# Recurrent kernel, one core: the next step's x gate goes into the PSUM sum from ScalarE in two halves, and no longer from VectorE

## The reference, cut to what matters

```
x = x + L0(x, cond)                      # gate, see below
xw = einsum('ntd,dh->nth', x, Wx) + b
def step(h_prev, xw_t):
    h_next = tanh(xw_t + h_prev @ Wh)    # 512 steps, one after the other
    return h_next, h_next
x = x + L1(x)                            # all h of the scan
x = x + L2(x)                            # forget/input gates f, i, candidate c, two cumulative sums over time
x = x + L3(x, ...)                       # one 512x512 product and a rank-8 term for each sequence
```

## Time and profile before

| | us |
|---|---|
| median of 3 runs | 1370.43 |
| lowest and highest | 1368.74, 1372.99 |
| the profiled execution, its own time | 1372.59 |
| its span, first to last instruction | 1370.7 |
| PE busy in the span | 1340.4 |
| DVE busy | 1066.7 |
| POOL busy | 767.2 |
| ACT busy | 695.2 |

### The profile page before, as it was taken

One profiled execution on the slowest core, in us unless ns is written; L12 is line 12 of the kernel. 1 busy time (PEld: TensorE's weight loads), 2 busy tenths in 40 slices (PEclk: granted clock), 3 DMA queues, 4 the chain that ended last, 5 costly groups with the idle time before them and its releaser, 6 DMA issues. The chain is left out here.

```text
span 1370.7 us, 50350 instructions
## 1 busy us (share of the span) xinstructions
PE 1340.4 (98%) x21246; PEld 887.3 (65%) x21246; DVE 1066.7 (78%) x2912; ACT 695.2 (51%) x2228; POOL 767.2 (56%) x620
## 2 busy tenths in 40 slices
PE   8999999999999999999999999999999997999998
PEld 6656666666666666666666666666666644677776
DVE  5756878777777777777777787878777888998993
ACT  4388555555555555555555555555545442333332
POOL 3255655464646464545555555554535557887884
PEclk9999999999999999999999999999999998999999
DMA  9771333333434242424242424241416568999993
GB/s 374 271 264 37 64 65 64 64 64 68 69 63 71 57 78 55 74 56 72 56 80 54 81 49 80 48 72 26 71 25 119 143 146 167 330 325 335 329 323 119
DMA packets 442276, 168.13 MB, mean 123 GB/s; under 512 B 406449, under 2 KB 409649, under 8 KB 438850
## 3 DMA queue, kind: packets, MB, share of 16 engines
q1 hardware_dynamic: 441584, 164.53, 47.6%
q10 hardware_dynamic: 466, 0.38, 0.1%
HBM read 96.72 MB, written 68.16 MB: 120 GB/s over the span
## 5 line engine op out<-in xcount | busy, mean ns | idle before, releaser
L509 PEld LDWEIGHTS recb<-hs,scanS 128*128 128x128 f16 x16352 | 466.1, 96 | 148.2 <-DVE hs L1492 144.3
L509 PE MATMUL recb<-hs,scanS 128*128 128x32 f16 x16352 | 488.3, 176 | 4.6 <-DVE hs L1492 3.5
L763 ACT ACTIVATE hs<-pre 128x64 f16<-128x64 f32 x512 | 131.2, 256 | 489.0 <-DVE pre L1480 487.5
L1480 DVE TENSOR_REDUCE pre<-recb 128x64 f32<-128x128 f32 x511 | 148.9, 291 | 186.4 <-PE recb L509 184.3
L1295 DVE RECIPROCAL gates<-gates 128x64 f32<-128x64 f32 (+1 forms) x484 | 257.8, 555 | 0.4
L1053 POOL TENSOR_SCALAR hbuf<-hbuf,sup 128x512 f32<-128x512 f32 (+2 forms) x61 | 94.1, 1542 | 126.9 <-ACT hbuf L767 126.9
L1492 DVE TENSOR_TENSOR hs<-konst,hs 128x64 f16<-128x64 f32 x512 | 103.5, 202 | 61.5 <-ACT konst L764 49.5
L1068 POOL TENSOR_TENSOR xt<-xt,pout 128x512 f32<-128x512 f32 x64 | 75.5, 1179 | 126.4 <-DVE pout L1325 126.4
L1335 DVE TENSOR_TENSOR recb<-xw,recb 128x128 f32<-128x128 f32 x511 | 145.8, 285 | 0.1
L1061 POOL TENSOR_TENSOR gates<-gates 128x512 f32<-128x512 f32 x62 | 78.8, 1271 | 105.0 <-DVE gates L1295 103.7
L767 ACT ACTIVATE hbuf<-pre 128x64 f32<-128x64 f32 x512 | 122.5, 239 | 0.0
(11 more groups left out here) (252 smaller groups left out, 2725.7 us busy)
## 6 DMA issues: line engine op xcount, KB each, us to landing
xt<-in_x SPq DMA_DIRECT2D x64, 256.0 KB, 3.5
g_d<-gst SPq DMA_DIRECT2D x64, 256.0 KB, 4.2
n_d<-nst SPq DMA_DIRECT2D x64, 256.0 KB, 3.1
x_d<-xt SPq DMA_DIRECT2D x64, 256.0 KB, 3.3
out<-gates SPq DMA_DIRECT2D x63, 256.0 KB, 4.9
xt<-x_d SPq DMA_DIRECT2D x28, 512.0 KB, 6.1
stage<-in_w SPq DMA_DIRECT2D x11, 1024.0 KB, 6.8
xt<-g_d SPq DMA_DIRECT2D x14, 512.0 KB, 8.0
```

The lines of the kernel that those rows point to most:

```text
L509: last = nc.tensor.matmul(sums[t % 2][:, m].rearrange("p a b -> p (a b)"), w[:, k, m * P:(m + 1) * P], hs[:, k].rearrange("p a b -> p (a b ...
L763: nc.scalar.activation(hs[:, :, 0, :], pre[t % 2][:], ACT.Tanh, scale=unscale).then_inc(s_h, 1)
L1480: nc.vector.tensor_reduce(pre[t % 2][:], sums[t % 2].rearrange("p c a b -> p c b a"), axis=AX.X, op=ALU.add).then_inc(s_pre, 1)
```

## The change

ScalarE gets a function `seed(n)`, called between its second and its third tanh of step n - 1. It writes half the gate of step n into both halves of the sum region (an ACTIVATE with Copy and scale 0.5), so their sum is again the gate, and raises a new semaphore `s_seed`. PE's step waits for it behind `s_hs`. VectorE's `seed`, the pair `halves`, its two memsets and their semaphore go. The input products of a block (`input_products`, chunk 0) get a wait that the gates they overwrite have been read. The seed waits, once in most blocks, for DVE's read of `bounds` in the same bank.

```diff
             def step(j, t):
                 pe.wait_ge(s_hs, TS * j + t + 1)
+                pe.wait_ge(s_seed, TS * j + t)
...
         @block.scalar
+            def seed(n):
+                if n == T:
+                    return
+                if n == 1:
+                    act.wait_ge(s_rec, 1)
+                if n % TS == 0:
+                    act.wait_ge(s_xw, C * (n // TS + 1))
+                if n - 1 == BOUND_FIRST:
+                    act.wait_ge(s_bd, 1)
+                elif n - 1 == BOUND_C:
+                    act.wait_ge(s_bd, 9)
+                elif TS < n < T - 2 * TS and (n - 1) % TS == BOUND_STEP:
+                    act.wait_ge(s_bd, 8 * (n // TS + 1) + 1)
+                gate = xw[n // TS % 2][:, n % TS].unsqueeze(2).to_broadcast([P, C, 2, B])
+                nc.scalar.activation(sums[n % 2], gate, ACT.Copy, scale=0.5).then_inc(s_seed, 1)
+
             def tanh(j, t):
...
                 nc.scalar.activation(hps, pre[t % 2][:], ACT.Tanh, scale=unscale).then_inc(s_h, 1)
+                seed(TS * j + t + 1)
                 if t % OCT == 0 and o >= RING:
                     act.wait_ge(s_x2, o - RING + 1)
                 nc.scalar.activation(hbuf[:, t % (RING * OCT)], pre[t % 2][:], ACT.Tanh, scale=unscale).then_inc(s_hb, 1)
...
             def input_products(q, m):
                 act.wait_ge(s_xp, C * q + m + 1)
                 if q >= 2 and m == 0:
+                    act.wait_ge(s_seed, TS * (q - 1) - 1)
                     act.wait_ge(s_bd, known(q) if q > 2 else 8)
...
         @block.vector
-            def seed(j, t):
-                j, t = j + t // TS, t % TS
-                if j == NBLK:
-                    return
-                if t == 0 and j:
-                    dve.wait_ge(s_xw, C * (j + 1))
-                gate = xw[j % 2][:, t].unsqueeze(2).to_broadcast([P, C, 2, B])
-                keep = halves.unsqueeze(1).unsqueeze(3).to_broadcast([P, C, 2, B])
-                nc.vector.tensor_tensor(sums[t % 2], gate, keep, ALU.mult)
...
                         nc.vector.tensor_tensor(pre[0][:], xw[0][:, 0], h0wh[:], ALU.add).then_inc(s_pre, 1)
-                        dve.wait_ge(s_rec, 1)
-                        nc.vector.memset(halves[:, 0:1], 1.0)
-                        nc.vector.memset(halves[:, 1:2], 0.0).then_inc(s_halves, 1)
-                        dve.wait_ge(s_halves, 1)
                     else:
                         dve.wait_ge(s_rec, TS * j + t + 1)
                         nc.vector.tensor_reduce(pre[t % 2][:], ...).then_inc(s_pre, 1)
-                    seed(j, t + 1)
```

More of the change, by code:

```diff
@@ L174, in build @@
         turned = recb[:, 2 * P:3 * P]
-        halves = recb[:, 2 * P:2 * P + 2]
         by_batch = turned.rearrange("p (c b) -> p c b", c=C)[:, :, 0:B]
@@ L224, in build @@
                                     "s_hyp s_lr").split())
-        (s_x1, s_x1h, s_x1l, s_xp, s_xw, s_rec, s_halves, s_pre, s_h, s_hb, s_hs, s_x2, s_x2h, s_x2l, s_lowd, s_f, s_i, s_c, s_fs, s_is, s_gs, s_r, s_fr,
+        (s_x1, s_x1h, s_x1l, s_xp, s_xw, s_rec, s_seed, s_pre, s_h, s_hb, s_hs, s_x2, s_x2h, s_x2l, s_lowd, s_f, s_i, s_c, s_fs, s_is, s_gs, s_r, s_fr,
          s_in, s_g, s_n, s_zero, s_car, s_P, s_X) = (
-            sem("r_" + s) for s in ("s_x1 s_x1h s_x1l s_xp s_xw s_rec s_halves s_pre s_h s_hb s_hs s_x2 s_x2h s_x2l s_lowd s_f s_i s_c s_fs s_is s_gs s_r s_fr "
+            sem("r_" + s) for s in ("s_x1 s_x1h s_x1l s_xp s_xw s_rec s_seed s_pre s_h s_hb s_hs s_x2 s_x2h s_x2l s_lowd s_f s_i s_c s_fs s_is s_gs s_r s_fr "
                                     "s_in s_g s_n s_zero s_car s_P s_X").split())
```

## The result

The changed kernel takes 1372.70 us (median of 18 runs, 1370.85 to 1375.73) and the kernel before 1370.21 us (18 runs beside them, 1368.74 to 1373.45). The ratio is 1.0018, with a 95% interval of 1.0011 to 1.0025: 2.5 us or 0.18% slower, inside the 0.3% that was set as no change. The forecast was 1372.8.

A forecast was written before the change was run, and what follows sets the result against it. PE, busy without holes at 2.10 us a step, was taken to bound the kernel and hide the chain. Terms -0.1 + 0.4 + 1.2 + 0.5 + 0.4 = +2.4 us gave 1372.8 us, range 1369.2 to 1378.0.

The forecast's parts named there:

- The seed's price and deadline: ScalarE's seed takes 0.27 us, 0.21 of ScalarE's time; beyond 0.33 it would hold up PE in some 480 paced steps.
- the lead: How early PE's weight load starts before its matmul in paced steps; 0.07 us of it can be lost for nothing.
- t = 3 overruns, blocks 2 to 14: ScalarE full at t = 3, next tanh 0.16 late, PE waits 0.09 in each of 13 blocks: 1.2 us.
- block 1, four steps: ScalarE full at t = 3, 4, 6, 8 of block 1, 0.12 lost each: 0.5 us.
- block 0, t = 19 and 24: ScalarE already at full overlap in these chain-bound steps, 0.21 lost each: 0.4 us.
- chain-bound steps, 35: Steps in blocks 0, 1 and 15 where PE waits for the chain; load 0.01 us later in each: 0.4 us.
- block 15, late VectorE items: A few late VectorE items in block 15 end some hundredths earlier: about -0.1 us in all.
- delayed ScalarE items that others wait for: GpSimd gets `hbuf` 0.21 us later and x2 casts wait at worst as long; products read them later: 0.
- The order of PE's waits: Dearer wait before PE's load: on the seed, load 0.01 us later; on the subtraction, 0.05 later, 1.8 us in chain-bound steps.
- VectorE as the pace: Rival: in 12 of 32 steps VectorE's chain pushes PE, so 168 steps gain 0.07 us each: 1361 us; chance 0.05.
- The seed as the bound: Rival: a seed over 0.33 us holds PE in every step; at 0.39, 1406 us; chance 0.11.
- More overruns: Rival: activations around the Copy do not overlap, 19 full ScalarE steps each lose 0.12 us more: 1376.5 us; chance 0.12.

The follow-up runs named there:

- (2): Kernel before with VectorE's seed taken out and nothing in its place: 1370.32 us, ratio 1.0002.
- (5, 6): Kernel before (5) and changed kernel (6), each with five instead of six filler matmuls a step in blocks 1 to 14: 1347.35 us and 1343.44 us.
- (1): Changed kernel with ScalarE's seed moved behind the third tanh: 1412.16 us, ratio 1.0302.
- (3): Kernel before, VectorE still seeding, with an extra unread ScalarE Copy of 128x128 into SBUF between second and third tanh: 1371.91 us, ratio 1.0009.
- (9): Changed kernel with chunk 3's forget share at t = 5 (blocks 2 to 14) and, at t = 15 of block 15, the seed behind the third tanh: 1371.91 us.
- (4): Changed kernel with PE's two waits in the other order, seed first and subtraction second: 1376.80 us, ratio 1.0041.
- (7): Changed kernel with ScalarE writing the whole gate into half 0 alone, 64 elements: 1373.05 us, ratio 1.0017.

## Why the prediction was right

**What bounds the steps.** Right, and shown from two sides. With VectorE's seed gone (2) nothing is won; with one filler less (5, 6) the same change is 3 to 4 us faster, though not by the 12 that the prediction named for the case without cover, since the chain-bound steps and the overruns take most of it back. The two chain lengths read from the rows, 2.014 and 2.087, came out as 2.013 and 2.087.

**The seed's price and deadline.** Predicted 0.27 and 0.21 of ScalarE's time; measured 0.262 and 0.20. The limit of 0.33 for its length was not run into by a longer seed but by a later one (1): the load follows the seed's end by 0.11, and the loss of 0.078 a paced step is about what 0.146 of delay leaves after the lead. The lead is 0.095 - 0.03 = 0.065, not 0.07.

**The sum by its terms**, for the stretch:

| term | predicted | measured |
|---|---|---|
| t = 3 overruns, blocks 2 to 14 | 1.2 | 0.60 (13 x 0.046) |
| block 1, four steps | 0.5 | 0.42 |
| block 0, t = 19 and 24 | 0.4 | 0.44 |
| chain-bound steps, 35 | 0.4 | 0.2 (0.013 in some 15 of them, about nothing in the others) |
| block 15, late VectorE items | -0.1 | -0.09 |
| delayed ScalarE items that others wait for | 0 | 0.20 + 0.24 (t = 6 of block 0, t = 17 of block 15) |
| sum | 2.4 | 2.0; the stretch has 2.1, most of the rest is t = 30 of block 0, where PE waits for a DMA |

The first tanh is late in just the 19 steps that the prediction named, but errors of size cancelled in part. The overruns of the steady blocks were put at twice what they cost: the tanh was 0.135 late and not 0.16, and a tanh that starts behind a busy ScalarE reaches the subtraction in 0.38 to 0.39 instead of 0.40, so 0.11 arrives at PE, of which the lead takes 0.065. The chain-bound term was twice too large as well: the 35 were counted by a load that starts with its matmul, but in 7 of them (t = 1, 2, 3, 5, 6, 15 and 30 of block 0) the load comes 0.10 to 1.0 after the subtraction, for other reasons. Why only some 15 of the other 28 pay the 0.013 was not looked for. And the step "GpSimd gets `hbuf` 0.21 later ... 0" failed at two places. In step t = 5 of block 0 the cast of x1hi stands 0.20 later, GpSimd's subtraction waits for it and PE for that, which makes t = 6 0.20 longer here, and 0.21 with ScalarE's time alone (3):

```profile
43.98 0.60 ACT L790 CAST x1hi<-xt 128x512 fp32r<-128x512 f32 x1
...
44.66 1.26 POOL L1052 TENSOR_TENSOR x1lo<-xt,x1hi 128x512 fp32r<-128x512 f32 x1 [0.77 <-ACT x1hi L790]
...
46.07 0.47 PE L545 MATMUL bank<-x1hi,wx_hi 128*128 128x512 f32 x1 [0.91 <-POOL x1lo L1052]
```

The cast starts 0.65 after the first tanh at 43.33; before, it was 0.45 (42.38 to 42.83). In block 15 the later `hbuf` moves GpSimd's add, which holds a VectorE operation and with it the reduction: 0.24, shown by (9).

**The order of PE's waits.** Taken from PE's first step as one of two bounds, and right: (4) measures 0.06 between the two. But the reason for the 0.01 was not separated in the prediction, and my later guess (the wait itself) was wrong: (7) shows that it is the seed's end, which stands 0.11 ahead of the load where the subtraction's stands 0.05. The prediction had the load 0.01 late. It is not; the same 0.013 comes behind the load.

**The rivals.** VectorE as the pace: excluded by (2). The seed as the bound: not at 0.262, but 0.15 later it is, at 1412 us. More overruns: its condition is not met, since the next activation starts 0.20 after the Copy and not 0.27; the worst single step costs 0.24. The upper end of the range should have read 1378.5 and not 1378.0 by the working given (1376.5 + 2). That the sum came within 0.1 us of the medians is luck in part: the medians' ratio is uncertain by 0.07%, 1 us. The tail's share in the 2.5 us can't be told from the profiles.

The formula of the Trainium skill's page "ScalarE: Activation LUTs" ("What ACT_TABLE_LOAD costs") gives an estimate of 0.29 us for this activation, and the copy into SBUF (3) takes 0.29. The page also says that PSUM is quicker than SBUF, without a number; the trace agrees, with 0.26. Its rule to put multiplications on VectorE, which it gives with bf16 in view, did not decide here: 262 ns on ScalarE against 285 on VectorE, in float32.

## What to carry to other kernels

When an engine is relieved, first look whether the pacing engine's instructions stand at their own distance already: if they do, the relief is worth nothing until that engine has less to do, and then it may be worth several us. Moving work costs at the few steps where the receiving engine's list is full, so read its idle time at each step and spread the list (0.6 us back here for one moved item). Where an instruction waits for two semaphores, write first the wait that ends last, and count who starts later by the moved work, through other engines too.

## What the runs showed of the hardware that was not expected

- A load behind two waits starts 0.054 us after the end of the instruction whose semaphore was waited for first in the code, and 0.113 to 0.115 after the one waited for second (in the changed kernel 0.054 and 0.113 in the same chain-bound steps; with the order turned 0.115 after the subtraction). The second wait is an instruction of its own on the load's queue, 51 ns long, 496 of them at the line of the seed's wait in the changed kernel:

```profile
L499 PEldq EVENT_SEMAPHORE  x496: 51/51/51, 32.6 to 1104.2; - x166
```

- A VectorE operation of 0.27 to 0.28 us on SBUF took 1.25 to 1.54 us beside a GpSimd add and ended 0.14 to 0.16 after it, in three kernels (the kernel before, the changed one, and (9)). The page "SBUF — State Buffer" of the Trainium skill, section "Who interferes with whom", has the rule: a VectorE instruction with two SBUF inputs contends with a GpSimd instruction that reads SBUF, over a shared port pair that one of them holds exclusively. The traces agree: this operation reads two SBUF tiles, and GpSimd's add had begun first each time. I had not applied the rule to a start that moves.
- ScalarE's Copy of 128x128 takes 0.262 us into PSUM and 0.29 into SBUF, but the next activation starts 0.20 after it in both cases: where ScalarE is full, the destination saves nothing.
